# Language-model tower: the second token span's rule lookups, counts and slots moved, its groups one step later, batch 3 projected later

## The chip, the cores and the metric

The kernel runs on one core of a Trainium2 chip. The metric is the device time of one execution in microseconds, as the median of several runs. TensorE does the matrix products, VectorE (DVE) the elementwise work and reductions, ScalarE (ACT) the exponentials and most copies out of PSUM, GpSimd (POOL) the indirect DMAs and some sums, SyncE (SP) issues most of the plain DMAs.

## The reference

Tokens x [8, 512] become a hidden state h [8, 512, 64] in three layers:

```python
h = einsum('bsd,bsde->bse', emb[x], rule_transform[token_rules[x]])   # 100 rules of 64x64
xn = layernorm(h)
h = h + attention(xn)     # 8 heads, rank 32 queries and keys, values are xn, no mask, out by VO [8,64,64]
h = h + moe(layernorm(h)) # 8 experts, hidden 128, relu, the two best gates, softmax of these two
```

The layernorms have no weights. The attention is softmax(q k^T / 8) over all 512 tokens of a batch.

## The kernel before, in words

**The rules.** The token's own 64x64 matrix is the costly part of the first layer. So tokens are sorted by rule on the chip. There are NC = 32 chunks of 128 tokens (four to a batch) in NQ = 4 quarters of QC = 8 chunks. Two spans are sorted apart: span 0 is quarter 0 (batches 0 and 1), span 1 the quarters 1 to 3 (batches 2 to 7). For each quarter q:

- `fetch` (line 514, GpSimd) gathers the embedding rows with their rule number into `etok`, which lies in the tile `ctxT`; semaphore `e_got[q]`.
- `look(i, q)` (line 757, VectorE, a generator with three yields) takes the rule numbers, builds the one-hot table `oh` and each token's rank within the span.
- `count` (line 1037, TensorE) adds up `oh` over the span's chunks into two PSUM banks.
- `starts` (line 781) turns the totals into the first slot of each rule, `slots(i, q)` (line 791) gives each token its slot in `pos` (`pos_ok`), and `tile_rules` (line 814) gives the rule of each tile of 64 slots, which TensorE turns into a row (`rule_row`, line 1049) from which it reads the addresses of the matrices (`trow_ok`).
- `place` (line 520, GpSimd) scatters the rows to their slots in HBM (`emb_sorted`), waiting after every fourth for the landing.

The sorted rows come back in groups of 512 slots, 15 groups for span 0 and 19 for span 1, loaded in pairs (`load_pair`). Each group is transposed (`turn`, line 1070), copied by ScalarE to `eT`, multiplied by its rule matrices (`apply`, line 1079) and copied to `y_out`, stored, and gathered back in token order into `hbuf` (`bring`, line 532). Span 0's groups run in a loop of their own (lines 1099 to 1110 on TensorE, 843 to 848 on VectorE). Span 1's groups run inside the attention of batch 0, at the steps that `R_AT` (line 246) lists.

**The attention.** Loops over b from -2 to 8 and k from 0 to 15 make the steps (b, k), and every engine walks them in the same order. In a step TensorE computes two tiles of transposed scores (line 1193, ScalarE's exponentials behind them at line 650), two tiles of scores of a later batch for the row maxima (line 1213, VectorE's reduction at line 961), the weighted sum P.V (line 1227) and the small work that `aux_at(b, k)` lists: the transpose of the layernorm's result (`xT`), the projections (`proj`), the transposes of the maxima (`mt`), the output projection (`vo`), the experts. The maxima run LEAD = 12 steps ahead: batch nb's first two tiles stand in step (nb-1, 4). The row of negated maxima goes through SyncE's `max_row` (line 451) into row 96 of the queries, so that the transposed scores come out shifted.

**Order around the change.** Batch nb's projections are written to `qk_h` and `qk_l`, one copy for all batches; SyncE's `stack` (line 438) spreads them by DMA into `qs` and `ks`. ScalarE may overwrite `qk_h` only when all stacks of the batch before have landed (lines 711 to 714). SyncE issues in a written order (lines 463 to 487); for b = 1: the sums' row, stack(2,3), max_row(1,1), stack(3,0), stack(3,1), max_row(2,0), stack(3,2). GpSimd issues in a written order too (lines 545 to 577): fetches, scatters of span 0, fetches, `bring(0,0)`, scatters of span 1 around `values(0)`, then loads and stores of span 1's groups with `bring(0,1)` between them, and `bring(1,2)`, `bring(1,3)` behind the last store. VectorE takes the layernorm of batch 1, 2 and 3 in portions from the steps (0,0), (0,10) and (0,14) on; each begins with a wait for `hbuf` (`y_loaded`).

Of the kernel before, what the change touches and what calls it, by code (L numbers as in the profile page):

```python
# [44 lines left out]
def lm_tower_kernel(nc, ids_in, table, rules, weights, consts, out, dims):  # L45
# [33 lines left out]
    with ctx:  # L79
# [166 lines left out]
        R_AT = [(-1, 14), (-1, 15)] + [(0, g // 3) for g in range(18)]  # L246

        def x_at(nb):

            return {1: (0, 2), 2: (0, 13)}.get(nb, (nb - 2, XT))  # L250

        def proj_at(nb):

            return {1: ((0, 2), (0, 2), (0, 3), (0, 3)), 2: ((0, 14), (0, 14), (0, 15), (0, 15))}.get(
                nb, [(nb - 2, k) for k in PROJ])

        def aux_at(b, k):
# [20 lines left out]
            if k == MT[0] and 0 <= b + 1 < B:  # L278
                todo.append(("mt", b + 1, 0))
# [231 lines left out]
        def _(pool):  # L511
# [33 lines left out]
            fetch(range(FIRST + 10))  # L545
            pool.wait_ge(S["zeroed_0"], 16 * 3)
            place(0, range(FIRST))
            for c in range(FIRST + 10, NC):
                fetch((c,))
                if c % 4 == 3:  # L550
                    pool.wait_ge(e_got[c // QC], 16 * (c % QC + 1))
# [4 lines left out]
            bring(0, 0)  # L556
            pool.wait_ge(S["zeroed_1"], 16 * 4)
# [4 lines left out]
            for n in range(NP0, len(PAIRS) + AHEAD):  # L562
# [4 lines left out]
                if n == NP0 + 2:  # L567
                    bring(0, 1)
# [157 lines left out]
        def _(dve):  # L726
# [51 lines left out]
            cum, tot = bank[4][:, 0:NR], bank[5][:, 0:NR]  # L778
            more, ends, first, key = (cnt[:, i, :] for i in range(4))

            def starts(i):

                dve.wait_ge(S["ranked"], i + 1)
                link(V.tensor_scalar(cnt_i[:, 0, :], tot, 1.0, -1.0, ALU.max, ALU.add))
# [6 lines left out]
            def slots(i, q):  # L791
# [4 lines left out]
                link(V.tensor_tensor(sel[:], oh[:, c0 - lo:c1 - lo, :], key.unsqueeze(1).to_broadcast([128, QC, NR]), ALU.mult))  # L796
                link(V.tensor_reduce(slot_f[:], sel[:], AX.X, ALU.add))
                link(V.tensor_tensor(both, slot_f[:], rank[:, c0:c1], ALU.add))
                link(V.tensor_scalar(nth, both, SHIFT, (B * T >> SHIFT) - 1, ALU.logical_shift_right, ALU.bitwise_and))
                link(V.tensor_scalar(ahead, both, (B * T).bit_length() - 1, None, ALU.logical_shift_right))  # L800
                link(V.tensor_scalar(at_in, both, TS - 1, 2, ALU.bitwise_and, ALU.logical_shift_left))
                link(V.tensor_tensor(past, nth, ahead, ALU.add))
                link(V.scalar_tensor_tensor(gap, past, float(NR - 1), rule_i[:, c0:c1], ALU.add, ALU.subtract))
                link(V.scalar_tensor_tensor(past, nth, 1.0, gap, ALU.min, ALU.mult))
                link(V.tensor_tensor(tile_, past, rule_i[:, c0:c1], ALU.add))
                link(V.tensor_scalar(hi, tile_, 2, None, ALU.logical_shift_right))
# [7 lines left out]
            def tile_rules(i):  # L814
# [5 lines left out]
                V.tensor_copy(trow[:, i, :], bank[5][0:1, 0:128]).then_inc(S["trow_ok"], 1)  # L820
# [8 lines left out]
            slots(0, 0)  # L829
            tile_rules(0)  # L830
            run(look(1, 1))
# [10 lines left out]
            later = chain(look(1, 2), look(1, 3))  # L842
            for g in range(NG[0]):
# [3 lines left out]
                if 5 <= g < 9 or g >= 11:  # L847
                    next(later, None)
            run(later)
            starts(1)  # L850
            slots(1, 1)
            slots(1, 2)

# [86 lines left out]
            for b in range(-2, B + 1):  # L940
                if b == -2:
                    run(layernorm(0, "xn_ready"))
                for k in range(16):

                    if (b, k) == (-2, 9):
                        slots(1, 3)
                        tile_rules(1)
                    if k == 0 and 0 <= b - 2 < LAST - 1:
# [7 lines left out]
                    for nb, u in s_units(b, k):  # L956
# [4 lines left out]
                        V.tensor_reduce(mx[:, u // 16, u % 16:u % 16 + 1], bank[3 + n % 2][:], AX.X, ALU.max).then_inc(S["mx_done"], 1)  # L961
                    for a in aux_at(b, k):
# [70 lines left out]
        def _(pe):  # L1033
# [3 lines left out]
            def count(i, q):  # L1037
# [5 lines left out]
                for c in range(q * QC, (q + 1) * QC):  # L1043
                    M(bank[4][:, 0:NR], before[:], oh[:, c - lo, :], start=c == lo, stop=c == hi - 1)
                    last = M(bank[5][:, 0:NR], ones_bf[:], oh[:, c - lo, :], start=c == lo, stop=c == hi - 1)
# [3 lines left out]
            def rule_row(i):  # L1049

                pe.wait_ge(S["trule_ok"], i + 1)
                M(bank[5][0:1, 0:128], trule[:], ident, start=True, stop=True).then_inc(S["trowed"], 1)
# [46 lines left out]
            for g in range(NG[0] + 1):  # L1099
# [9 lines left out]
                if g in (8, 11, 13):  # L1109
                    count(1, (8, 11, 13).index(g) + 1)  # L1110
            pe.wait_ge(S["y_ok"], NG[0])

# [163 lines left out]
```

## Time and profile before

| | us |
|---|---|
| median of 3 runs | 634.21 |
| lowest, highest | 631.71, 635.44 |
| the profiled execution | 635.93 |
| its span in the trace | 633.8 |
| TensorE busy | 509.3 (80%) |
| VectorE busy | 417.5 (66%) |
| ScalarE busy | 284.7 (45%) |
| GpSimd busy | 231.3 (36%) |

The profiled execution's own time is 2.1 us more than its span. The chain that ended last goes through TensorE for 52% of the span, VectorE for 14%, GpSimd for 12% and DMAs for 7%. In the rows below the first number of a timeline row is its start and the second its length, both in us; a bracket at the end is the engine's idle time just ahead of it and what ended it.

### The profile page before, as it was taken

The page shows a single profiled execution, that of the slowest core. Times are in us where ns is not written, and L with a number is a line of the kernel's source. Part 1 is how long each engine was busy: PE and PEld are TensorE (multiplying, and loading weights), DVE is VectorE, ACT ScalarE, POOL GpSimd, SP SyncE. Part 2 cuts the span into 40 slices and gives each one's busy share as a digit, 9 for nine tenths or more (in the row PEclk, how much of TensorE's full clock was granted, in tenths as well). Part 3 has the DMA queues.
Part 4 walks back from the last instruction along what each step waited for, and adds up shares of the span by engine and source line. Part 5 has one row for each costly group of instructions (what it writes and reads, how often), then busy time and mean ns, then how long its engine had stood idle before and what let it go on. Part 6 is the DMA issues. An engine that isn't in the chain of part 4 may idle for free.

```text
span 633.8 us, 9445 instructions
## 1 busy us (share of the span) xinstructions
PE 509.3 (80%) x2732; PEld 276.6 (44%) x2732; DVE 417.5 (66%) x1026; ACT 284.7 (45%) x566; POOL 231.3 (36%) x379
## 2 busy tenths in 40 slices
PE   0178303867789897999999999999999899999684
PEld 0046301334444433445544544544554355757463
DVE  5633385734216955888778969868866876754666
ACT  0105001026555534465555565565465555386233
POOL 5764255563225200421451254133132322624512
PEclk9998655559679997999999999999999999999866
DMA  8735113733381071533320450422034000000000
GB/s 241 294 85 152 51 27 80 153 93 99 84 234 42 14 170 41 113 85 77 76 60 2 100 118 2 100 61 51 19 88 105 1 2 11 1 10 10 1 9 8
DMA packets 21935, 47.05 MB, mean 74 GB/s; under 512 B 6264, under 2 KB 11720, under 8 KB 21824
## 3 DMA queue, kind: packets, MB, share of 16 engines
q1 hardware_dynamic: 15552, 32.23, 21.0%
q0 software_dynamic: 4752, 8.20, 5.0%
q10 hardware_dynamic: 1584, 6.03, 2.9%
q8 instruction: 25, 0.41, 0.3%
q14 instruction: 22, 0.18, 0.1%
HBM read 9.97 MB, written 11.01 MB: 33 GB/s over the span
## 4 chain that ended last, share of the span: by engine, by line
PE 52%; DVE 14%; POOL 12%; issue 9%; DMA 7%; ACT 2%; SPq 2%; DVEq 0%; ACTq 0%; POOLq 0%
PE bank L1227 14%; PE bank L1213 10%; PE bank L1193 7%; POOL emb_sorted L527 5%; PE bank L1155 5%; POOL ctxT L517 4%; PE bank L1177 4%; DVE mx L961 3%; DMA ctxT<-in_table,ids 2%; PE bank L1149 2%; PE bank L1085 2%; PE bank L1150 2%; DVE r_sb L1008 2%; POOL r_sb L591 2%; DMA emb_sorted<-ctxT,pos 1%
## 5 line engine op out<-in xcount | busy, mean ns | idle before, releaser
L961 DVE TENSOR_REDUCE mx<-bank 128x1 f32<-128x512 f32 x256 | 170.5, 687 | 85.5 <-PE bank L1213 82.5
L591 POOL TENSOR_TENSOR r_sb<-r_sb 128x256 f32<-128x256 f32 x180 | 93.5, 519 | 265.5 <-DVE r_sb L1026 171.0
L650 ACT ACTIVATE prob<-bank 128x512 f32<-128x512 f32 x256 | 138.7, 597 | 58.3 <-PE bank L1193 45.7
L1213 PE MATMUL bank<-ks,qs 96*128 96x512 f32 x256 | 123.2, 489 | 10.8 <-DVE mx L961 10.5
L1227 PE MATMUL bank<-prob,xa 128*64 128x512 f32 x448 | 124.0, 633 | 0.0
L1213 PEld LDWEIGHTS bank<-ks,qs 96*128 96x128 f32 x256 | 51.1, 200 | 127.5 <-issue 107.1
L1193 PE MATMUL bank<-qs,ks 97*128 97x512 f32 x224 | 78.6, 433 | 0.0
L708 ACT ACTIVATE r_sb<-bank,stay 128x512 f32<-128x512 f32 x56 | 37.1, 686 | 44.9 <-PE bank L1150 44.7
L1193 PEld LDWEIGHTS bank<-qs,ks 97*128 97x128 f32 x224 | 38.8, 196 | 15.3 <-issue 10.5
L517 POOL DMA_INDIRECT ctxT<-in_table,ids x32 | 32.5, 1017 | 23.9 <-DMA ctxT<-in_table,ids 11.2
L527 POOL DMA_INDIRECT emb_sorted<-ctxT,pos x32 | 33.5, 1047 | 20.1 <-DMA emb_sorted<-ctxT,pos 11.7
L1227 PEld LDWEIGHTS bank<-prob,xa 128*64 128x64 f32 x448 | 22.5, 137 | 39.3 <-issue 34.9
L535 POOL DMA_INDIRECT hbuf<-y_sorted,pos x32 | 31.3, 977 | 22.4 <-DMA y_sorted<-y_out 13.7
L1085 PE MATMUL bank<-r_sb,eT 128*64 128x64 f32 (+1 forms) x544 | 28.5, 260 | 12.4 <-DVE y_out L846 11.2
L1177 PE MATMUL bank<-stay,ctxT 128*128 128x128 f32 x256 | 35.4, 285 | 0.1
L1149 PE MATMUL bank<-xs,w_h 128*128 128x512 f32 (+1 forms) x72 | 31.7, 441 | 4.6 <-DVE r_sb L1008 3.4
L1177 PEld LDWEIGHTS bank<-stay,ctxT 128*128 128x128 f32 x256 | 34.0, 200 | 2.2 <-ACT negm L719 0.4
L714 ACT CAST qk_h<-bank 128x512 fp32r<-128x512 f32 x32 | 18.4, 587 | 30.8 <-PE bank L1137 23.8
L1013 DVE TENSOR_TENSOR qk_l<-bank,qk_h 128x512 fp32r<-128x512 f32 x32 | 21.7, 687 | 15.9 <-ACT qk_h L714 15.9
L1085 PEld LDWEIGHTS bank<-r_sb,eT 128*64 128x64 f32 x544 | 23.2, 165 | 20.0 <-issue 17.8
L1132 PE MATMUL bank<-cst,xn 128*128 128x128 f32 x64 | 10.7, 289 | 24.1 <-DVE xn L892 23.9
L1076 PE MATMUL bank<-cst,e_in 128*128 128x128 f32 x68 | 16.7, 338 | 16.3 <-DMA e_in<-emb_sorted 8.0
(161 smaller groups left out, 693.4 us busy)
## 6 DMA issues: line engine op xcount, KB each, us to landing
qs<-qk_h SPq DMA_DIRECT2D x64, 128.0 KB, 2.5
ks<-qk_h SPq DMA_DIRECT2D x56, 128.0 KB, 2.4
qs<-qk_l SPq DMA_DIRECT2D x32, 128.0 KB, 2.6
ks<-qk_l SPq DMA_DIRECT2D x28, 128.0 KB, 2.5
emb_sorted<-front ACTq DMA_DIRECT2D x4, 608.0 KB, 9.7
y_sorted<-y_out POOLq DMA_DIRECT2D x19, 128.0 KB, 2.2
e_in<-emb_sorted POOLq DMA_DIRECT2D x9, 256.0 KB, 3.3
emb_sorted<-front ACTq DMA_DIRECT2D x3, 640.0 KB, 9.5
```

Source lines behind the costliest of these rows:

```text
L517: nc.gpsimd.indirect_dma_start(etok[:, c, :], None, table, bass.IndirectOffsetOnAxis(ap=ids[:, 1, c:c + 1], axis=0)).then_inc(e_got[c // Q ...
L527: nc.gpsimd.indirect_dma_start(emb_sorted[i], bass.IndirectOffsetOnAxis(ap=pos[:, c:c + 1], axis=0), etok[:, c, 0:D], None).then_inc(S[f"s ...
L591: nc.gpsimd.tensor_tensor(a[:, at:at + width], src[:, 0:width], src[:, width:2 * width], ALU.add).then_inc(S["pool_chain"], 1)
L650: nc.scalar.activation(prob[:, step % NPROB, u % 2, :], bank[u % NST][:], ACT.Exp, scale=SC).then_inc(S["exp_done"], 1)
L708: nc.scalar.activation(hid_of(ab)[:, i, :], ring(a)[:, 0:x2_of(ab).shape[1]], ACT.Relu, bias=b1_f[:, i:i + 1]).then_inc(S["relu_done"], 1)
L961: V.tensor_reduce(mx[:, u // 16, u % 16:u % 16 + 1], bank[3 + n % 2][:], AX.X, ALU.max).then_inc(S["mx_done"], 1)
L1085: last = M(out_[half * TS:(half + 1) * TS, c * D:(c + 1) * D], eT[:, g % 2, col:col + TS], r_sb[:, at_:at_ + D] if isinstance(at_, int) el ...
L1149: M(o, w1_h[:, i * HID:(i + 1) * HID], x2, start=True, stop=False)
L1177: last = M(out_[:, pair * 128:(pair + 1) * 128], ctxT[:, b % 2, pair, i * 128:(i + 1) * 128], vo_blk[:, pair, :, :].rearrange("p t e -> p ...
L1193: last = M(bank[u % NST][:], keys[:, h, :], qs[:, ub % 2, h, :], start=True, stop=True)
L1213: M(bank[3 + n % 2][:], qs[0:96, nb % 2, h, tt * 128:(tt + 1) * 128], ks[0:96, nb % 2, h, :], start=True, stop=True).then_inc(S["s_ps"], 1)
L1227: last = M(bank[5][64 * hh:64 * hh + 64, :], xa[:, b % XAR, ut, :], prob[:, step, hh, :], start=(ut == 0), stop=(ut == J - 1))
```

## The change

Fetches: eight, a wait for their landing, six more, then span 0's scatters, then the other eighteen in batches that end at chunks 17, 21, 25, 29 and 31. `bring(0,1)` directly follows `bring(0,0)`. VectorE: look 1 leaves its place ahead of the weights and looks 1 and 2 are spread over the groups 2 to 5 and 8 on; look 3 follows the last group. `slots` becomes a generator; slots 2 is split over the steps (-2,1), (-2,2), (-2,5) and (-2,9), and slots 3 over the first reductions of maxima. TensorE counts quarters 1 to 3 behind all groups of span 0, into banks 0 and 1 in place of 4 and 5. Span 1's groups stand in (0,1) to (0,7) in place of (-1,14) to (0,5). The first half of batch 0's maxima is transposed in (-1,11), behind tile 16, in place of (-1,13). Batch 3's transpose stands in (1,7) in place of (1,4), and its four projections in (1,8) to (1,11) in place of (1,5) to (1,8).

```diff
-        R_AT = [(-1, 14), (-1, 15)] + [(0, g // 3) for g in range(18)]
+        R_AT = [(0, 1 + g // 3) for g in range(20)]
...
-            return {1: (0, 2), 2: (0, 13)}.get(nb, (nb - 2, XT))
+            return {1: (0, 2), 2: (0, 13), 3: (1, 7)}.get(nb, (nb - 2, XT))
...
-            return {1: ((0, 2), (0, 2), (0, 3), (0, 3)), 2: ((0, 14), (0, 14), (0, 15), (0, 15))}.get(
+            return {1: ((0, 2), (0, 2), (0, 3), (0, 3)), 2: ((0, 14), (0, 14), (0, 15), (0, 15)), 3: ((1, 8), (1, 9), (1, 10), (1, 11))}.get(
                 nb, [(nb - 2, k) for k in PROJ])
...
                 todo.append(("gate", b - 2, 0))
-            if k == MT[0] and 0 <= b + 1 < B:
+            if (b, k) == (-1, 11) or k == MT[0] and 0 <= b < B - 1:
                 todo.append(("mt", b + 1, 0))
...
-            fetch(range(FIRST + 10))
+            fetch(range(QC))
+            pool.wait_ge(e_got[0], 16 * QC)
+            fetch(range(QC, QC + 6))
             pool.wait_ge(S["zeroed_0"], 16 * 3)
             place(0, range(FIRST))
-            for c in range(FIRST + 10, NC):
+            for c in range(QC + 6, NC):
                 fetch((c,))
-                if c % 4 == 3:
+                if c % 4 == 1 or c == NC - 1:
                     pool.wait_ge(e_got[c // QC], 16 * (c % QC + 1))
...
             bring(0, 0)
+            bring(0, 1)
             pool.wait_ge(S["zeroed_1"], 16 * 4)
...
                     load_pair(pool, n)
-                if n == NP0 + 2:
-                    bring(0, 1)
                 for g in PAIRS[n - AHEAD] if n >= NP0 + AHEAD else ():
...
-            cum, tot = bank[4][:, 0:NR], bank[5][:, 0:NR]
             more, ends, first, key = (cnt[:, i, :] for i in range(4))
...
                 dve.wait_ge(S["ranked"], i + 1)
+                cum, tot = bank[4 - 4 * i][:, 0:NR], bank[5 - 4 * i][:, 0:NR]
                 link(V.tensor_scalar(cnt_i[:, 0, :], tot, 1.0, -1.0, ALU.max, ALU.add))
...
                 link(V.tensor_tensor(sel[:], oh[:, c0 - lo:c1 - lo, :], key.unsqueeze(1).to_broadcast([128, QC, NR]), ALU.mult))
+                yield
                 link(V.tensor_reduce(slot_f[:], sel[:], AX.X, ALU.add))
+                yield
                 link(V.tensor_tensor(both, slot_f[:], rank[:, c0:c1], ALU.add))
...
                 link(V.tensor_scalar(at_in, both, TS - 1, 2, ALU.bitwise_and, ALU.logical_shift_left))
+                yield
                 link(V.tensor_tensor(past, nth, ahead, ALU.add))
...
                 link(V.tensor_tensor(tile_, past, rule_i[:, c0:c1], ALU.add))
+                yield
                 link(V.tensor_scalar(hi, tile_, 2, None, ALU.logical_shift_right))
...
                 dve.wait_ge(S["trowed"], i + 1)
-                V.tensor_copy(trow[:, i, :], bank[5][0:1, 0:128]).then_inc(S["trow_ok"], 1)
+                V.tensor_copy(trow[:, i, :], bank[5 - 4 * i][0:1, 0:128]).then_inc(S["trow_ok"], 1)
...
             starts(0)
-            slots(0, 0)
+            run(slots(0, 0))
             tile_rules(0)
-            run(look(1, 1))
             dve.wait_ge(S["w_h"], 3)
...
-            later = chain(look(1, 2), look(1, 3))
+            later = chain(look(1, 1), look(1, 2))
             for g in range(NG[0]):
...
                 V.tensor_copy(y_out[:, g % 4, :], bank[2 + g % 2][:, 0:4 * D]).then_inc(S["y_ok"], 1)
-                if 5 <= g < 9 or g >= 11:
+                if 2 <= g < 6 or g >= 8:
                     next(later, None)
             run(later)
+            run(look(1, 3))
             starts(1)
-            slots(1, 1)
-            slots(1, 2)
+            run(slots(1, 1))
...
                     run(layernorm(0, "xn_ready"))
+                    later = slots(1, 2)
                 for k in range(16):
...
                     if (b, k) == (-2, 9):
-                        slots(1, 3)
+                        run(later)
                         tile_rules(1)
+                        later = slots(1, 3)
+                    if (b, k) in ((-2, 1), (-2, 2), (-2, 5)):
+                        next(later, None)
                     if k == 0 and 0 <= b - 2 < LAST - 1:
...
                         V.tensor_reduce(mx[:, u // 16, u % 16:u % 16 + 1], bank[3 + n % 2][:], AX.X, ALU.max).then_inc(S["mx_done"], 1)
+                        next(later, None)
                     for a in aux_at(b, k):
...
                 for c in range(q * QC, (q + 1) * QC):
-                    M(bank[4][:, 0:NR], before[:], oh[:, c - lo, :], start=c == lo, stop=c == hi - 1)
-                    last = M(bank[5][:, 0:NR], ones_bf[:], oh[:, c - lo, :], start=c == lo, stop=c == hi - 1)
+                    M(bank[4 - 4 * i][:, 0:NR], before[:], oh[:, c - lo, :], start=c == lo, stop=c == hi - 1)
+                    last = M(bank[5 - 4 * i][:, 0:NR], ones_bf[:], oh[:, c - lo, :], start=c == lo, stop=c == hi - 1)
                 if c == hi - 1:
...
                 pe.wait_ge(S["trule_ok"], i + 1)
-                M(bank[5][0:1, 0:128], trule[:], ident, start=True, stop=True).then_inc(S["trowed"], 1)
+                M(bank[5 - 4 * i][0:1, 0:128], trule[:], ident, start=True, stop=True).then_inc(S["trowed"], 1)
...
                     apply(g - 1, bank[2 + (g - 1) % 2])
-                if g in (8, 11, 13):
-                    count(1, (8, 11, 13).index(g) + 1)
             pe.wait_ge(S["y_ok"], NG[0])
+            for q in range(1, NQ):
+                count(1, q)
...
                                 pe.wait_ge(S["exp_done"], u - NST + 1)
+                            else:
+                                pe.wait_ge(S["trow_ok"], 2)
                             keys = ks[:, ub % 2, :, ut * 128:(ut + 1) * 128]
...
                                 h = 2 * pair + u % 2
...
```

## Rows read from the trace of the kernel before

**Rows 1.** Busy time by stretch: PE, PEld, DVE, ACT, POOL, then the granted clock and DMA.

```profile
135.00:204.00 69.00, 58.25 (x452) 32.03 (x454) 25.14 (x51) 38.97 (x91) 25.33 (x38) 0.83 0.43 116
...
250.00:530.00 280.00, 273.43 (x1234) 136.89 (x1234) 222.75 (x499) 155.89 (x290) 87.48 (x173) 1.00 0.27 61
```

**Rows 2.** Timeline of the first span's groups: VectorE's fourth lookup, TensorE's next group.

```profile
70.11 0.72 DVE L763 CAST rule<-ctxT 128x8 f32<-128x8 int32 x1 [11.17 <-DMA ctxT<-in_table,ids]
...
72.04 1.12 PE L1085 MATMUL bank<-r_sb,eT 128*64 x16 [10.69 <-DVE y_out L846]
```

**Rows 3.** Timeline, GpSimd: the last span-0 scatter, and first issues of two batches of fetches.

```profile
39.62 0.97 POOL L527 DMA_INDIRECT emb_sorted<-ctxT,pos  x1 [0.30 <-issue]
...
54.69 0.95 POOL L517 DMA_INDIRECT ctxT<-in_table,ids  x1 [3.07 <-DMA ctxT<-in_table,ids]
...
63.79 0.95 POOL L517 DMA_INDIRECT ctxT<-in_table,ids  x1 [4.37 <-DMA ctxT<-in_table,ids]
...
70.07 0.74 POOL L552 MEMSET xa<- 128x768 f32 x1 [1.57 <-DMA ctxT<-in_table,ids]
```

**Rows 4.** Timeline, VectorE, from the totals to the first reduction of maxima.

```profile
78.95 0.25 DVE L784 TENSOR_SCALAR cnt_i<-bank 128x100 int32<-128x100 f32 x1
...
85.73 0.99 DVE L796 TENSOR_TENSOR sel<-oh,cnt 128x800 f32<-128x800 bf16 x1
...
90.95 0.42 DVE L866 TENSOR_REDUCE ln_s<-hbuf 128x4 f32<-128x256 f32 x1
...
104.05 0.69 DVE L1013 TENSOR_TENSOR qk_l<-bank,qk_h 128x512 fp32r<-128x512 f32 x1 [0.16 <-ACT qk_h L714]
...
111.70 1.29 DVE L961 TENSOR_REDUCE mx<-bank 128x1 f32<-128x512 f32 x2 [0.45 <-PE bank L1213]
```

**Rows 5.** Timeline, GpSimd: scatter of chunk 16 and the loads of span 1's first groups.

```profile
100.89 0.97 POOL L527 DMA_INDIRECT emb_sorted<-ctxT,pos  x1 [1.45 <-DMA emb_sorted<-ctxT,pos]
...
131.49 2.25 POOL L393 DMA_DIRECT2D e_in<-emb_sorted  x3 [1.46 <-DMA emb_sorted<-ctxT,pos]
```

**Rows 6.** Timeline, TensorE: first group of span 1, first transposed scores.

```profile
134.89 0.66 PE L1076 MATMUL bank<-cst,e_in 128*128 128x128 f32 x2 [6.23 <-DMA e_in<-emb_sorted]
135.21 1.20 PE L1193 MATMUL bank<-qs,ks 97*128 97x512 f32 x2
```

**Rows 7.** Timeline, TensorE: P.V of the steps (0,1), (0,2), (0,6) and (0,7).

```profile
146.49 1.08 PE L1227 MATMUL bank<-prob,xa 128*64 128x512 f32 x4
...
153.13 1.08 PE L1227 MATMUL bank<-prob,xa 128*64 128x512 f32 x4
...
192.49 1.08 PE L1227 MATMUL bank<-prob,xa 128*64 128x512 f32 x4
...
194.64 1.08 PE L1227 MATMUL bank<-prob,xa 128*64 128x512 f32 x4
```

**Rows 8.** Timeline: last store of span 1, and VectorE's start of layernorm 2.

```profile
192.37 0.54 POOL L398 DMA_DIRECT2D y_sorted<-y_out  x1 [0.40 <-ACT y_out L676]
...
201.41 0.42 DVE L866 TENSOR_REDUCE ln_s<-hbuf 128x4 f32<-128x256 f32 x1 [0.23 <-DMA hbuf<-y_sorted,pos]
```

**Rows 9.** Timeline, TensorE and ScalarE: P.V of (1,6), (1,7), (1,8) and the stall.

```profile
234.22 1.08 PE L1227 MATMUL bank<-prob,xa 128*64 128x512 f32 x4
...
240.41 0.58 ACT L714 CAST qk_h<-bank 128x512 fp32r<-128x512 f32 x1 [6.97 <-DMA ks<-qk_l]
...
241.77 0.59 PE L1172 MATMUL bank<-cst,srow 8*128 8x8 f32 x4 [5.57 <-DVE qk_l L1013]
...
243.87 1.98 PE L1227 MATMUL bank<-prob,xa 128*64 128x512 f32 x4
...
247.97 1.08 PE L1227 MATMUL bank<-prob,xa 128*64 128x512 f32 x4
```

**Rows 10.** Timeline: SyncE's max row of batch 2, and the scores that need it.

```profile
263.49 0.52 SPq L454 DMA_DIRECT2D qs<-negm  x1
...
266.84 0.71 PE L1193 MATMUL bank<-qs,ks 97*128 97x512 f32 x2
```

## The prediction

> **What bounds the kernel now.** I read the page's forty slices first, then busy time by stretch, then the chain that ended last, then the timeline engine by engine. "Step (b,k)" is one pass of the loops over b and k; the weighted sum P.V (line 1227) runs once per step, so its starts are the clock hand of everything behind 135 us. "Maxima" are the tiles of line 1213 and their reductions of line 961.
>
> From 250 us on TensorE is busy 273 of 280 us at the full 2.4 GHz; from 135 to 204 it is busy 58 of 69 us at a granted 0.83 [rows 1]. So the steady part gives nothing back: what the change can win lies ahead of 250 us, and a gain there reaches the end only if it passes every later wait. In order of time there are five such places.
>
> - The span-0 groups stop for 10.7 us, because VectorE waits 11.2 us in the fourth lookup for `e_got[3]` with a finished group's copy behind it [rows 2].
> - VectorE runs starts, two slots and the first layernorm in a row up to 96 us, then the third slots and the tile rules behind the projections; the first reduction of maxima is at 111.70 [rows 4].
> - At (-1,14) TensorE waits 6.2 us for the second span's first rows; the first transposed scores start behind it at 135.21 [rows 6].
> - The last second-span group is stored at 192.37, and VectorE starts layernorm 2 in step (0,10) at 201.41, 0.2 us after it was free: this wait is just not late now [rows 8].
> - In step (1,5) ScalarE waits 7.0 us before it may overwrite `qk_h` for batch 3, since batch 2's stacks still read it; TensorE is idle 5.6 us and its next P.V takes 1.98 instead of 1.08 us, the mark of 1.2 GHz [rows 9].
>
> **Part 1, the fetches (GpSimd queue).** Before: 18 fetches, 8 scatters, 14 fetches in batches with a wait for landing. After: 14 fetches, 8 scatters, then 18 fetches in batches of 4, 4, 4, 4, 2. GpSimd is free earlier, so the scatters begin with `pos_ok` (28.7 us) and end some 0.6 us earlier than the 40.6 us that the last one's row gives [rows 3]. A batch with its landing takes 9.1 us (54.69 to 63.79) or, with the DMA engines nearly alone, 6.3 us (63.79 to 70.07) [rows 3]. I take the mean, 7.7: 40.3 + 4 x 7.7 = 71.1, then two issues (1.3) and a landing (3.5) give `e_got[3]` at 76 instead of 70. The ends are 40.3 + 4 x 6.3 + 4.8 = 70 and 40.3 + 4 x 9.1 + 4.8 = 81.5. This is the largest unknown, -6 to +5.5 us, and most of what follows shifts with it one for one.
>
> **Part 2, the first span.** The lookup steps now follow groups 2 to 5 and 8 on. The step behind group 5 ends look 1 and runs into look 2, which waits for `e_got[2]`: chunk 23 is issued near 58 us and lands near 61. So a stall stays, from about 54.8 to 61.3, 6.5 instead of 10.7 us. Nine groups follow, some at the slow pace of 1.7 us, the last at 1.05: copied out near 72.5 instead of 79. But nothing uses that directly: look 3 now starts with `e_got[3]` at 76. From there: look 3.3 us, the last count 0.6 behind it, starts 1.8 and one slots 5.2 (85.73 to 90.95 in rows 4) give 86.9, where layernorm 0 begins, against 90.95: 4.1 us earlier. `hbuf` is there in time (store of group 14 near 76, four gathers from 77.5, landed near 84). `bring(0,1)` goes from 134 to 83 us and costs nothing, since the scatters behind it need `pos_ok` at 87 anyhow.
>
> **Part 3, up to the first scores.** The four projections follow layernorm as before, so the last `qk_l` (104.05) comes at about 100.2. Two slots steps (2.0 us) lie where VectorE waited 1.9 us for ScalarE; ends -0.2 and +0.5 us, I take +0.1. The rest of slots 2 (2.0 us) and the tile rules (1.5) still stand ahead of the rule row, and the first stack lands 5 us behind the projections, so the first reduction starts near 106.7 instead of 111.70 [rows 4]. Slots 3 (5.2 us) are now spread over the first five reductions: these take 8.2 us, the next eleven 0.82 us each as now, and tile 16 is done near 123.9. The max row leaves at once, for its transpose now stands in (-1,11); its round trip (2.0 us of DMA) ends at 127, while TensorE does six tiles more (4.9 us) and starts the transposed scores near 129.2, against 135.21: 6.0 us earlier [rows 6].
>
> **Part 4, the groups one step later.** Scatter 16 leaves at 102.9 with `pos_ok` instead of 100.89, and by the same spacing of 30.6 us [rows 5] the first loads go at 133.5 and land near 137. TensorE comes to the first group in (0,1) near 138, so the 6.2 us wait is gone, with 1 us to spare (ends: 0 and 3 us of wait). But 5 of 20 group turns that stood ahead of P.V(0,1) now stand behind it, and the last stands in (0,7) behind two more plain steps of 2.15 us [rows 7]. In numbers: P.V(0,1) near 137.0 (part of it still at the slow clock); a step with three groups is 6.6 us (146.49 to 153.13), so P.V(0,2) is at 143.6; the same four steps with the same projections cost 39.4 (153.13 to 192.49), so P.V(0,6) is at 183.0 and P.V(0,7) at 189.6; two turns more, and the last store goes near 192.8, against 192.37 [rows 8]. So the 6.0 us are spent: layernorm 2 starts at 201.8 and not 201.41, +0.4 us. What is late next is the same wait: VectorE reaches (0,10) near 198 and now waits 3 to 4 us there, with the reductions of (0,10) queued behind it and TensorE behind these.
>
> **The clock.** Behind 5.6 us of idle TensorE ran at 1.2 GHz for about one step and a half [rows 9]. Behind the new wait of 3 to 4 us I take 1.5 us of loss, with ends 0 (clock stays) and 3 (two steps at 4.3 instead of 2.7, as VectorE is the slower there). The Trainium skill, "TensorE: Matmul & The Clock Gate", section "HAM oscillation — how this bites in real kernels", speaks against this part of the change: waits for data between bursts bring the array back to half rate each time. By it the upper end would hold, and the sum would be 1.5 us less good. The trace agrees for the wait of 5.6 us; it has no wait of 3 to 4 us between dense stretches.
>
> **Part 5, batch 3 projected later.** Its transpose goes from (1,4) to (1,7), its projections from (1,5..8) to (1,8..11). P.V(1,6) to P.V(1,8) takes 13.75 us now [rows 9]; two plain steps with the rt transposes and the batch transpose are 2 x 2.15 + 0.5 + 0.35 = 5.2, and the projection work of 0.55 a step is only moved. So 8.1 us go. The stacks land at 240.3; without the stall (1,8) is reached near 240, so ends 0 and 1 us of rest. What is late next: `qk_lo` of batch 3 then comes 8.4 us ahead of (1,15), and SyncE must issue twelve stack DMAs (7.5 us) before it sends the max row, which takes 0.5 + 1.8 us. The scores of (1,15) wait for it, while today the row left at 263.49 for a start at 266.84 [rows 10]. I take 1.3 us (0 to 3). Part 5 is -6.8, between -4 and -8.
>
> **Sum.** +0.4 (layernorm 2) + 1.5 (clock) - 6.8 = -4.9 us against the profiled execution's 635.93: 631.0. That execution lies 1.7 above the median of 634.21, on which a new median will be measured, so I predict 629.4 us.
>
> **The rivals.**
> - Early fetches, 625: batches cost 6.3 us, as with quiet DMA engines, and the maxima are less DVE-bound. Layernorm 2 starts 4 to 6 us earlier. For it: the first batches run while VectorE stalls the stores; against: the one batch beside stores took 9.1. Chance 0.20.
> - Late groups, 633.5: batches cost 8.5 to 9, or the first span-1 loads are late, and layernorm 2 starts 4 us later, giving back the half of part 5. Chance 0.22.
> - The edit of part 5 doesn't clear the stall, because batch 2's stacks are later against (1,8) or ScalarE's wait only moves: half of 8.1 stays, 633.4. It is for that the stacks need SyncE's 24 issues, against it the 240.3 landing. In the 0.22 above.
> - Slower, 638: the clock in batch 0. From 135 to 204 TensorE is busy 58 us at a mean of 0.83, which is 48 us of work at 2.4 GHz [rows 1]. The turns stand in steps as dense as before, but ahead of them the steps (0,0) and (0,1) are thinner; if the clock stays down longer, at a mean of 0.73, the same 48 us take 66, 8 us more. Then layernorm 2 starts 8 us later: -4.9 + 8 = +3. It decides from 7 us on, when all of part 5 is eaten. Against it: from (0,1) on three turns a step follow each other as they do now. Chance 0.10.
> - The forecast, 627 to 632: 0.48.
>
> **How the numbers follow.** Shifting the fetches between their ends gives 629.4 - 6 = 623.4 and 629.4 + 5.5 = 634.9; with the clock's and part 5's ends added in part I say 622.5 to 635.5, leaving the slow-clock case out above. 0.5% is 3.2 us, about what a measurement can tell: below 631.0 is faster. Early fetches (0.20) and five sixths of the forecast (0.40) are there; the late groups' lower tail adds a little: 0.62 faster, 0.28 same, 0.10 slower.
>
> **What the changed profile would show.** `e_got[3]` (VectorE's fourth lookup) at 76, a VectorE stall behind group 5 near 55 to 61, layernorm 0 at 87, the first reduction near 107, the first transposed scores near 129 with no 6 us wait, the last group store near 193, a VectorE wait on `hbuf` in (0,10), no wait of ScalarE on `ks<-qk_l` behind 235, and a short wait ahead of the scores of (1,15). If `e_got[3]` is at 70 or 82, if the last store is off 192.8 by more than 3 us, or if a wait on the stacks stays, the prediction is wrong there.

## The result: slower by 0.6%, and what the profile after shows

| | before | after |
|---|---|---|
| median of 20 runs each | 635.78 | 637.57 |
| lowest, highest | 629.32, 646.58 | 634.30, 642.99 |
| ratio after / before, 95% interval | | 1.0063 (1.0040 to 1.0085) |
| profiled execution, its span | 635.93, 633.8 | 635.24, 633.4 |

The ratios here and below are taken without disturbed (slow) runs, of which before had more, while medians are of all runs: these differ by only 1.8 us, 0.3%. The forecast was 629.4, between 622.5 and 635.5. The two traces end within 0.4 us of each other, so the loss itself is not in this pair of traces; where the expected gain went can be read from it.

Busy time by stretch (as [rows 1]): from 135 to 204 TensorE is busy 5.6 us less than before, at a granted clock of 0.90 against 0.83 (part of the smaller busy time is that clock itself); from 204 to 250 the clock is 0.85 against 0.93 before.

```profile
135.00:204.00 69.00, 52.64 (x448) 28.09 (x444) 23.15 (x48) 37.43 (x89) 22.64 (x34) 0.90 0.39 109
204.00:250.00 46.00, 38.95 (x139) 17.88 (x139) 29.59 (x61) 20.23 (x39) 4.63 (x6) 0.85 0.32 73
250.00:530.00 280.00, 271.95 (x1227) 136.23 (x1225) 221.77 (x497) 155.90 (x291) 88.09 (x174) 1.00 0.27 61
```

VectorE's timeline through the span-0 groups and after them (answers [rows 2] and [rows 4]): look 2 waits only 1.0 us, the last group's copy is at 74.02 and look 3 right behind it; layernorm 0 starts at 84.59 instead of 90.95, the first reduction of maxima at 106.03 instead of 111.70.

```profile
59.49 0.17 DVE L764 CAST rule<-ctxT 128x8 f32<-128x8 int32 x1 [1.00 <-DMA ctxT<-in_table,ids]
...
74.02 0.42 DVE L850 COPY y_out<-bank 128x256 f32<-128x256 f32 x1 [0.42 <-PE bank L1094]
74.36 0.16 DVE L764 CAST rule<-ctxT 128x8 f32<-128x8 int32 x1
...
84.59 0.42 DVE L870 TENSOR_REDUCE ln_s<-hbuf 128x4 f32<-128x256 f32 x1
...
106.03 0.69 DVE L969 TENSOR_REDUCE mx<-bank 128x1 f32<-128x512 f32 x1 [3.71 <-PE bank L1224]
```

GpSimd (answers [rows 3] and [rows 5]): a fetch batch takes 6.6 us (55.63 to 62.26), not 7.7; the fetches have landed at 72.58. Scatter 16 and the first loads:

```profile
55.63 0.95 POOL L517 DMA_INDIRECT ctxT<-in_table,ids  x1 [1.73 <-DMA ctxT<-in_table,ids]
...
62.26 0.95 POOL L517 DMA_INDIRECT ctxT<-in_table,ids  x1 [1.90 <-DMA ctxT<-in_table,ids]
...
72.58 0.74 POOL L554 MEMSET xa<- 128x768 f32 x1 [1.46 <-DMA ctxT<-in_table,ids]
...
101.33 0.96 POOL L527 DMA_INDIRECT emb_sorted<-ctxT,pos  x1 [2.21 <-DVE pos L816]
...
129.98 2.94 POOL L393 DMA_DIRECT2D e_in<-emb_sorted  x4 [1.47 <-DMA emb_sorted<-ctxT,pos]
```

TensorE (answers [rows 6] and [rows 7]): the first transposed scores stand at 127.66 instead of 135.21, the first group without a wait, then P.V of (0,1), (0,2), (0,7) and (0,8).

```profile
127.66 1.05 PE L1204 MATMUL bank<-qs,ks 97*128 97x512 f32 x2
...
134.49 1.08 PE L1238 MATMUL bank<-prob,xa 128*64 128x512 f32 x4
...
135.83 0.60 PE L1085 MATMUL bank<-cst,e_in 128*128 128x128 f32 x4
...
139.81 1.08 PE L1238 MATMUL bank<-prob,xa 128*64 128x512 f32 x4
...
183.63 1.08 PE L1238 MATMUL bank<-prob,xa 128*64 128x512 f32 x4
...
187.90 1.08 PE L1238 MATMUL bank<-prob,xa 128*64 128x512 f32 x4
```

The last store and layernorm 2 (answers [rows 8]): the store is 4.6 us earlier than before. VectorE's wait ahead of layernorm 2 is 4.57 instead of 0.23 us; TensorE waits 4.64 us behind it, and its next P.V takes 1.97 instead of 1.08 us.

```profile
187.78 0.54 POOL L398 DMA_DIRECT2D y_sorted<-y_out  x1 [0.40 <-ACT y_out L677]
...
196.86 0.42 DVE L870 TENSOR_REDUCE ln_s<-hbuf 128x4 f32<-128x256 f32 x1 [4.57 <-DMA hbuf<-y_sorted,pos]
...
198.81 0.57 PE L1224 MATMUL bank<-ks,qs 96*128 96x512 f32 x1 [4.64 <-DVE mx L969]
199.31 1.97 PE L1238 MATMUL bank<-prob,xa 128*64 128x512 f32 x4
```

Batch 1 (answers [rows 9] and [rows 10]), TensorE's P.V of (1,6), the scores of (1,7), P.V of (1,7) and (1,8), the scores of (1,15); then SyncE's two max rows:

```profile
229.56 1.08 PE L1238 MATMUL bank<-prob,xa 128*64 128x512 f32 x4
...
236.74 1.22 PE L1204 MATMUL bank<-qs,ks 97*128 97x512 f32 x2 [5.29 <-DMA qs<-negm]
...
238.32 1.98 PE L1238 MATMUL bank<-prob,xa 128*64 128x512 f32 x4
...
243.08 1.98 PE L1238 MATMUL bank<-prob,xa 128*64 128x512 f32 x4
...
266.68 0.73 PE L1204 MATMUL bank<-qs,ks 97*128 97x512 f32 x2 [1.01 <-DMA qs<-negm]
...
228.33 1.35 SPq L470 DMA_DIRECT2D srow<-ctxT  x2
...
234.08 0.59 SPq L448 DMA_DIRECT2D ks<-qk_l  x1
234.72 0.59 SPq L454 DMA_DIRECT2D qs<-negm  x1
...
264.50 0.59 SPq L454 DMA_DIRECT2D qs<-negm  x1
```

Here is the answer. ScalarE's wait for the stacks is gone, as forecast, but the scores of (1,7) wait 5.29 us for `qs<-negm`: max row (1,1), which SyncE can send only behind batch 2's 24 stack DMAs and the sums' row. Before, SyncE issued the same row at 238.56:

```profile
238.56 0.59 SPq L454 DMA_DIRECT2D qs<-negm  x1
```

With the 1.98 us that such a row takes to land it stood ready at 240.5, while TensorE was held until 241.77 by `qk_h`. There were two waits of nearly one length, one behind the other's back. The changed kernel's chain that ended last says it in order of time: it runs through SyncE's issues from 221 to 234.7.

```profile
220.30 0.60 ACT prob L651
221.34 0.59 SPq L445
...
227.69 0.59 SPq L448
228.33 0.70 SPq L470
229.07 1.86 DMA srow<-ctxT
...
234.72 1.98 DMA qs<-negm
236.74 1.22 PE bank L1204 x2
```

### The profile page after: what moved, and what is told of

It reads as the page before. It is cut to its first block, busy times and chain, and to the rows that moved or that the text cites. A ratio compares the mean times of both kernels' runs of the same rounds, so it can differ in the third digit from the quotient of the medians.

```text
span 633.4 us, 9456 instructions
## 1 busy us (share of the span) xinstructions
PE 509.5 (80%) x2732; PEld 275.7 (44%) x2732; DVE 416.8 (66%) x1026; ACT 285.0 (45%) x566; POOL 231.7 (37%) x379
## 4 chain that ended last, share of the span: by engine, by line
PE 56%; DVE 18%; issue 9%; DMA 5%; POOL 5%; SPq 3%; ACT 3%; another core or an unknown queue 1%; ACTq 0%; DVEq 0%; POOLq 0%
PE bank L1238 14%; PE bank L1224 11%; PE bank L1204 7%; PE bank L1164 5%; DVE mx L969 4%; PE bank L1186 4%; PE bank L1094 3%; PE bank L1158 2%; PE bank L1159 2%; DVE r_sb L1017 2%; PE bank L1085 2%; SPq L445 2%; SPq L448 2%; POOL r_sb L592 2%; DMA ks<-qk_l 2%
## 5 line engine op out<-in xcount | busy, mean ns | idle before, releaser
L1238 PE MATMUL bank<-prob,xa 128*64 128x512 f32 x448 | 125.3, 639 | 0.0
L517 POOL DMA_INDIRECT ctxT<-in_table,ids x32 | 32.8, 1024 | 23.5 <-DMA ctxT<-in_table,ids 11.1
L1094 PE MATMUL bank<-r_sb,eT 128*64 128x64 f32 (+1 forms) x544 | 27.1, 251 | 10.7 <-ACT eT L634 6.2
L1094 PEld LDWEIGHTS bank<-r_sb,eT 128*64 128x64 f32 x544 | 22.1, 158 | 18.3 <-issue 9.5
L1164 PE MATMUL bank<-r_sb,stay 128*64 128x512 f32 x112 | 27.8, 606 | 1.6 <-ACT r_sb L709 1.0
L1159 PE MATMUL bank<-xs,w_l 128*128 128x512 f32 (+1 forms) x72 | 28.2, 393 | 0.0
```

The source lines that it names most:

```text
L1094: last = M(out_[half * TS:(half + 1) * TS, c * D:(c + 1) * D], eT[:, g % 2, col:col + TS], r_sb[:, at_:at_ + D] if isinstance(at_, int) el ...
L1159: M(o, w1_l[:, i * HID:(i + 1) * HID], x2, start=False, stop=True).then_inc(S["up_ps"], 1)
L1164: last = M(out_[64 * t:64 * t + 64, 0:x2_of(b).shape[1]], w2_f[:, 2 * i + t, :], hid_of(b)[:, 2 * i + t, :], start=True, stop=True)
L1238: last = M(bank[5][64 * hh:64 * hh + 64, :], xa[:, b % XAR, ut, :], prob[:, step, hh, :], start=(ut == 0), stop=(ut == J - 1))
```

## The experiments

Times are against the kernel before in the same comparison, as medians, with the ratio and its interval. Two kernels of different comparisons are set against each other only by way of their own "before beside it".

| kernel | median | before beside it | ratio (95%) |
|---|---|---|---|
| batch 3's move alone | 634.05 | 634.74 | 0.990 (0.980 to 0.999), from 3 of its 6 runs |
| the same again | 634.81 | 632.71 | 1.003 (1.000 to 1.007) |
| changed, without batch 3's move | 634.94 | 634.74 | 1.002 (0.998 to 1.006) |
| changed, again | 637.44 | 634.74 | 1.004 (1.000 to 1.007) |
| before, again | 633.50 | 632.62 | 1.002 (0.999 to 1.005) |
| changed, row (1,1) first | 630.89 | 634.74 | 0.994 (0.991 to 0.997) |
| before, batch 3's move and row first | 627.32 | 632.71 | 0.991 (0.989 to 0.994) |
| changed, row first, groups one step earlier | 623.06 | 632.71 | 0.985 (0.982 to 0.989) |
| the same, row (2,0) early too | 623.10 | 632.71 | 0.986 (0.983 to 0.989) |
| changed, row first, key stacks by GpSimd | 632.69 | 632.62 | 0.999 (0.995 to 1.003) |
| changed without batch 3's move, key stacks by GpSimd | 633.95 | 632.62 | 1.004 (1.001 to 1.007) |
| before, key stacks by GpSimd | 633.17 | 632.62 | 0.997 (0.993 to 1.001) |

From the traces, three marks: P.V of (0,0), the start of layernorm 2, and the stretch from there to P.V of (2,4), all in us.

| trace | P.V (0,0) | layernorm 2 | from there to P.V (2,4) |
|---|---|---|---|
| before | 140.2 | 201.4 | 77.1 |
| before, again | 137.9 | 200.8 | 76.8 |
| batch 3's move alone | 135.1 | 193.4 | 79.0 |
| the same again | 137.7 | 203.6 | 78.6 |
| before, batch 3's move and row first | 136.9 | 197.5 | 73.8 |
| changed | 130.8 | 196.9 | 81.4 |
| changed, again | 131.9 | 198.1 | 82.3 |
| changed, without batch 3's move | 130.4 | 199.9 | 78.1 |
| changed, row first | 131.7 | 200.2 | 74.7 |
| changed, row first, groups one step earlier | 130.8 | 198.4 | 72.1 |
| the same, row (2,0) early too | 132.0 | 194.6 | 72.5 |
| changed, row first, key stacks by GpSimd | 132.5 | 201.0 | 74.5 |
| changed without batch 3's move, key stacks by GpSimd | 131.5 | 200.7 | 78.7 |

From P.V (2,4) to the end all of them take 353.5 to 356.8 us, so what is won or lost up to there reaches the end.

**Batch 3's move alone**, twice.

```diff
-            return {1: (0, 2), 2: (0, 13)}.get(nb, (nb - 2, XT))
+            return {1: (0, 2), 2: (0, 13), 3: (1, 7)}.get(nb, (nb - 2, XT))
...
+            ... 3: ((1, 8), (1, 9), (1, 10), (1, 11))}.get(
```

> The kernel before with the move of batch 3 alone (its transpose in (1,7), its projections in (1,8) to (1,11)). Theory A, the prediction's part 5: ScalarE's wait for the stacks in (1,5) was the stall, so it goes and the time falls by 4 to 8 us. Theory B, from the changed kernel's trace: behind it stands a second wait of nearly the same length, the scores of (1,7) for the max row (1,1), which SyncE sends behind batch 2's 24 stack DMAs; the old stall only covered it and gave cover to the projections beside it. Then TensorE waits 4 to 5.5 us in (1,7) for the row, three projections and a max-row wait of about 1 us come on top in (1,8) to (1,15), and the time is 0 to 3 us above the kernel before.

> The kernel before with batch 3's move alone, once more, since its first time was uncertain (interval 0.980 to 0.999) and its trace had started layernorm 2 at 193.4 us on code that is that of the kernel before. By the traces the stretch from layernorm 2 to P.V of (2,4) is 79.0 against 77.0 us, so 1 to 3 us above the kernel before. If it is 3 us or more below, batch 3's move does win something that the traces' stretches don't show.

TensorE of the first of the two:

```profile
226.04 1.08 PE L1227 MATMUL bank<-prob,xa 128*64 128x512 f32 x4
...
233.27 1.22 PE L1193 MATMUL bank<-qs,ks 97*128 97x512 f32 x2 [5.25 <-DMA qs<-negm]
...
234.85 1.98 PE L1227 MATMUL bank<-prob,xa 128*64 128x512 f32 x4
...
238.84 1.08 PE L1227 MATMUL bank<-prob,xa 128*64 128x512 f32 x4
...
253.82 0.47 PE L1213 MATMUL bank<-ks,qs 96*128 96x512 f32 x1 [0.73 <-DVE mx L961]
...
260.80 0.72 PE L1193 MATMUL bank<-qs,ks 97*128 97x512 f32 x2 [1.06 <-DMA qs<-negm]
```

On the code of before, the move alone makes the 5.25 us wait for the max row in (1,7), the 0.73 us wait for VectorE and the 1.06 us wait in (1,15). The stretch is 79.0 and 78.6 against 77.1 and 76.8: the move costs 1.9 us in the mean. The first time, by its ratio some 6 us below before, would even fit theory A, but it rests on three runs; the second gives a loss of 0.3%, with an interval (0.9998 to 1.0065) that just includes none. The first trace started layernorm 2 at 193.4, on code that is that of before up to there. So the times of this kernel decide little. Theory A falls by the traces, in which the scores of (1,7) wait 5.25 and 5.31 us, and by the next experiment.

**The changed kernel without batch 3's move** (the same lines the other way).

> The changed kernel with batch 3's transpose and projections back where they were. Theory A: the stall of (1,5) comes back and the time rises by 4 to 8 us over the changed kernel. Theory B: SyncE's issues set the end of that stretch either way, so the upstream lead of 3.7 us at P.V of (1,0) is now kept to the end: 1 to 4 us below the changed kernel and 0 to 3 us below the kernel before. P.V of (1,6) to (1,7) takes near 9.7 us, and no wait for the max row stands ahead of the scores of (1,15).

ScalarE's timeline of this kernel, then TensorE's, in batch 1:

```profile
240.16 0.58 ACT L715 CAST qk_h<-bank 128x512 fp32r<-128x512 f32 x1 [7.43 <-DMA ks<-qk_l]
...
241.52 0.59 PE L1181 MATMUL bank<-cst,srow 8*128 8x8 f32 x4 [6.03 <-DVE qk_l L1022]
```

The old stall is back, and the time falls by 2.5 us against the changed kernel beside it (634.94 against 637.44), where theory A wanted it 4 to 8 us higher. So the move costs some 2 to 2.5 us, and all the other changes together come out at the level of before: 1.002. It isn't 0 to 3 us below before, as I expected; the lead of 3.7 us in the first trace was not typical.

**The row ahead of stack(2,3).**

```diff
+                if b == 1:
+                    max_row(b, 1)
                 if 0 <= b + 1 < B:
                     stack(b + 1, 3)
-                if 0 <= b < B:
+                if 0 <= b < B and b != 1:
                     max_row(b, 1)
```

> The changed kernel, with SyncE sending max row (1,1) ahead of stack(2,3) instead of behind it. Theory B: the row leaves near 231 instead of 234.7, so the scores of (1,7) wait 1 to 2 us instead of 5.3; stack(2,3) lands 2 to 3 us later, near 239, which ScalarE may feel for up to 2 us in (1,8). 1 to 3 us below the changed kernel. Rival: the wait is not the row but the stacks' landing, then nothing changes or it gets slower by the 2 us.

SyncE's timeline of this kernel (the sums' row, then max row (1,1)), then TensorE's:

```profile
231.84 1.35 SPq L470 DMA_DIRECT2D srow<-ctxT  x2
234.46 0.56 SPq L454 DMA_DIRECT2D qs<-negm  x1
...
236.33 0.88 PE L1206 MATMUL bank<-qs,ks 97*128 97x512 f32 x2 [1.37 <-DMA qs<-negm]
```

One small DMA moved ahead of six others on one queue: the wait is 1.37 us instead of 5.29, no wait on the stacks shows, and the kernel is 6.5 us below the changed one beside it. That is more than twice the 3 us that I expected at most, and it matches the stretch (74.7 against 81.4 and 82.3): the wait is 3.9 us shorter, and the granted clock is 0.50 from some 237 to 240 only, against 233 to 247 in the changed kernel's first trace. The order on SyncE's queue is shown to be the cause. What is left of the wait comes from the sums' row: SyncE sends the max row only when that row, issued at 231.84, has landed.

**The same on the kernel before**, with batch 3's move (both edits above).

> The kernel before with batch 3's move and with max row (1,1) ahead of stack(2,3), but with nothing of the other changes. If the upstream changes win nothing at the end (theory C), this equals the changed kernel with the row sent first, that is 3 to 5 us below the kernel before, or is up to 1.5 us better. If the upstream lead is real and kept, it is 3 to 4 us above that kernel.

5.4 us below before, and 1.5 us better against its own neighbour than the row with all the upstream changes (3.9): the upper end of what theory C gave. So the upstream changes, as they stand, win nothing.

**Both kernels again**, unchanged, for a second trace.

> The changed kernel once more, for a second trace and for its time beside the others of this comparison: 0 to 4 us above the kernel before. Open is where the time differs from one execution to the next, since the two first traces have spans within 0.4 us of each other. If the lead at layernorm 2 (196.9 against 201.4 us) is typical, it is there again within 1 us; the rival is that the first trace was a lucky one and layernorm 2 starts at 199 or later.

> The kernel before once more, for a second trace. The lead of the changed kernel at layernorm 2 (its two traces: 196.9 and 198.1 us) was taken against one trace of before, 201.4. The kernel with batch 3's move alone has the same code up to there and started layernorm 2 at 193.4. So I expect 193 to 202 here: near 193 to 198 says that the changed kernel has no lead there as a rule, near 201 that it has one of about 3 us.

The changed kernel's second trace starts layernorm 2 at 198.1, between the two cases that I had set (within 1 us of 196.9, or 199 and later). Before's second trace starts it at 200.8, which by my own expectation spoke for a lead of 3 us; with all traces taken together there is none. The mark of layernorm 2 on code with the upstream part of before: 201.4, 200.8, 193.4, 203.6, 197.5, mean 199.3. With the changed upstream part: 196.9, 198.1, 199.9, 200.2 and, in two further traces, 201.0 and 200.7, mean 199.5. At the first P.V the lead is there in every trace (137.6 against 131.5 in the mean, 6 us), at layernorm 2 the means are equal. The single traces lie between 193.4 and 203.6 and between 196.9 and 201.0, so five and six of them can't exclude a difference of 2 or 3 us; the times of the kernel without batch 3's move (1.002) and of the one above speak against a lead.

**Groups one step earlier.**

```diff
-        R_AT = [(0, 1 + g // 3) for g in range(20)]
+        R_AT = [(0, g // 3) for g in range(20)]
```

> The changed kernel with max row (1,1) sent first, and span 1's groups in (0,0) to (0,6) instead of (0,1) to (0,7). Theory C: in every trace of the changed upstream part VectorE waits 4.4 to 4.6 us in (0,10) for hbuf, because the last group stands two plain steps later; the lead of 6 us at the first P.V is spent there, and TensorE comes out of it at the slow clock. One step earlier the last store comes about 2 us earlier, the wait falls to 0.5 to 2.5 us, and the time is 1 to 3 us below the kernel with the row sent first alone. Rival: the loads land too late for (0,0) (133.3 us against 132), so that step takes the wait, the clock falls there, and nothing is won.

VectorE's and TensorE's timeline of this kernel at layernorm 2:

```profile
198.35 0.42 DVE L872 TENSOR_REDUCE ln_s<-hbuf 128x4 f32<-128x256 f32 x1 [2.42 <-DMA hbuf<-y_sorted,pos]
...
200.31 0.47 PE L1226 MATMUL bank<-ks,qs 96*128 96x512 f32 x1 [2.49 <-DVE mx L971]
```

The wait at (0,10) is 2.4 instead of 4.6 us, and the time is 9.7 us below before (623.06, ratio 0.985): better than both kernels. Against the row first alone, each by its own before, it is 5.8 us better, where I expected 1 to 3. In this trace and that of the next experiment layernorm 2 starts at 198.4 and 194.6 (mean 196.5, against 199.5), and from there to P.V (1,0) it takes 17.7 us in both, against 18.3 to 21.5 with the later groups. That is some 4 of the 5.8 us, from two traces and across two comparisons; the rest I can't place. P.V (1,6) to (1,8) took 6.7 us here, as the clock stayed at 1.00 behind the wait for the row, but 8.3 in the next experiment's trace and 8.2 with the later groups: this is no gain of the edit. The loads don't hold the first group at (0,0): it starts at 133.6 with no wait of note. ScalarE waits 1.88 us for a stack in (1,8), which holds up nothing that shows.

**Row (2,0) early too.** `max_row(2, 0)` is moved ahead of `stack(3, 1)`.

> As the groups one step earlier with row (1,1) first, and in addition SyncE sends max row (2,0) ahead of stack(3,1). The wait of 1.0 us ahead of the scores of (1,15) goes: 1 us below that kernel, 4 to 7 us below the kernel before. If stack(3,1) is now late for anything, it shows as a wait on ks in (2,12) and the gain is gone.

The wait at (1,15) is gone from the trace and the step is 1.2 us shorter, P.V (1,14) to (1,15) being 3.0 instead of 4.2. The median is the same, 623.10, and so is the stretch, 72.5 against 72.1, since this trace has the slow clock behind the wait in (1,7) and the other hasn't. 1 us is below what six runs can tell, so the edit is unproven.

**Key stacks by GpSimd**, in three kernels.

```diff
-                for s, src in enumerate((qk_h, qk_h, qk_l) if b else ()):
+                for s, src in enumerate((qk_h, qk_h, qk_l) if b and b != 2 else ()):
...
+                if b == 0:
+                    pool.wait_ge(S["qk_lo"], 12)
+                    for g in range(4):
+                        pool.wait_ge(S["exp_done"], 8 * (g + 1))
+                        for s, src in enumerate((qk_h, qk_h, qk_l)):
+                            pool.dma_start(ks[32 * s:32 * s + 32, 0, 2 * g:2 * g + 2, :].bitcast(F32),
+                                           src[32 * g:32 * g + 32, 2:4, :].bitcast(F32)).then_inc(key_in[g], 16)
...
```

> The changed kernel with max row (1,1) ahead of stack(2,3), and batch 2's twelve key stacks issued by GpSimd, which has nothing to do there, instead of by SyncE. If SyncE's issues are what sets the stretch from P.V (1,6) to (1,8), the scores of (1,7) wait under 1 us (5.3 in the changed kernel, 1.4 with the row first alone) and ScalarE waits for no stack in (1,8): 5 to 9 us below the changed kernel. Rival: the 128 KB stacks are limited by their transfer and not by who issues them; then it is level with the row sent first alone, 6 to 7 us below the changed kernel, or GpSimd's own order delays it to a loss.

> The changed kernel without batch 3's move, and with batch 2's key stacks issued by GpSimd. Batch 2's stacks have landed near 236 instead of 240, so ScalarE's wait in (1,5) falls from 7 to 2 or 3 us: 4 to 6 us below the same kernel with SyncE issuing all. Rival as before: nothing changes if the transfer and not the issue is the limit.

> The kernel before with nothing changed but batch 2's key stacks issued by GpSimd. The double stall of (1,5) and (1,7) had one cause, 24 issues on one queue, so half of the issues taken away shortens both: 4 to 6 us below the kernel before. If it is level with the kernel before, the two waits aren't set by SyncE's issues.

All three missed: the times are within 0.4% of before, and the kernel with the row first isn't better for it (0.999, against 0.994 without). SyncE's timeline of that kernel while batch 2's stacks are sent, and GpSimd's line behind its twelve stacks:

```profile
224.32 1.90 SPq L446 DMA_DIRECT2D qs<-qk_l  x1
226.27 4.21 SPq L446 DMA_DIRECT2D qs<-qk_h  x2
230.53 2.02 SPq L446 DMA_DIRECT2D qs<-qk_l  x1
...
227.76 1.03 POOL L538 DMA_INDIRECT hbuf<-y_sorted,pos  x1 [0.30 <-issue]
```

Busy time of both kernels from 224 to 228 (columns as in [rows 1]; first with GpSimd, then with the row first alone):

```profile
224.00:228.00 4.00, 4.00 (x16) 1.75 (x16) 3.62 (x8) 1.72 (x4) 3.70 (x9) 1.00 0.95 197
```

```profile
224.00:228.00 4.00, 4.00 (x16) 1.62 (x16) 3.04 (x5) 2.31 (x5) 0.39 (x1) 1.00 0.85 197
```

GpSimd sends its twelve in 5.9 us, but SyncE's own issues stretch meanwhile: two of them take 4.21 us where they take 1.2 otherwise. In the stretch in which both queues send nothing but stacks, the DMA engines move 197 GB/s with one queue and with two; they are busy 0.85 of the time with SyncE alone, and 0.95 with both. That speaks for the rival of the first expectation, that the transfer and not the issue is the limit. The wait for the row is 1.36 us with GpSimd (and 0.77 for the sums' row just ahead of it) and 1.37 without, and the stretches to P.V (2,4) are level (74.5 and 74.7). Without batch 3's move, ScalarE's wait for the stacks is 5.68 instead of 7.43 us, so there they did land earlier, but two P.V behind it take 1.98 us instead of one, and the stretch is 78.7 against 78.1.

The test isn't clean. GpSimd works in a written order, so the edit also holds back the four gathers of `hbuf` that stand behind the stacks: they are issued at 227.8 to 232.6, beside the stacks, instead of 210.7 to 215.4. From 228 to 232 the engines move 262 GB/s with them against 210 without. What twelve issues on a second queue would bring without the gathers was not tried.

## Why the prediction was wrong, step by step

- **Part 1, fetches.** `e_got[3]` forecast at 76, landed at 72.5 (72.4 to 75.3 in the other traces of this code). The batch read above cost 6.6 us, near the lower end of 6.3. VectorE reached look 3 only at 74.36, behind the last group, which had been forecast at 72.5: two waits changed places, and layernorm 0 came at 84.6 to 86.6 in six traces against 86.9. Right in size.
- **Parts 2 and 3.** First reduction 106.0 (forecast 106.7), first transposed scores 127.7 (129.2), the 6 us wait at (-1,14) gone. Right; the lead at the first P.V is real in every trace.
- **Part 4.** "The 6.0 us are spent": layernorm 2 forecast 0.4 us later than before, found 0.2 us later in the mean of the traces. The first trace alone, 4.6 us earlier and with its last store at 187.8 instead of 192.8, would have called this wrong by the prediction's own sign. The new wait was forecast at 3 to 4 us and is 4.4 to 4.6. Not forecast was a wait of TensorE for a stack ahead of the maxima between P.V (0,3) and (0,4): 1.5 to 3.1 us in all six traces with the groups one step later, none in the two with the groups one step earlier. Three of the five traces with the upstream code of before have such a wait too (1.6 to 2.4 us), but not the one on which the prediction was built.
- **The clock.** Forecast 1.5 us. From layernorm 2 to P.V (1,0) the two traces of before take 17.65 us each, five of the six with the later groups 18.3 to 19.1 and the sixth 21.5: 1.4 us more in the mean. Right in size. The upper end of 3 us, which the forecast had tied to a rule of the Trainium skill ("TensorE: Matmul & The Clock Gate", section "HAM oscillation — how this bites in real kernels"), that waits for data between bursts bring the array back to its slow rate, was reached once in six. What the rule says of the single wait holds here: 1.97 instead of 1.08 us for the P.V behind the 4.64 us wait.
- **Part 5 is the step that failed.** The forecast took 8.1 us off and put back 1.3 for the max row of (1,15). That row's wait was right (1.01 us). (8.1 is not quite its own difference: 13.75 less 5.2 is 8.55.) But the stretch P.V (1,6) to (1,8) was priced as 5.2 us of plain steps, as if nothing else were late there. The text asked what is late next for (1,15) and not for (1,7), where the same queue holds max row (1,1) behind the same stacks. Measured with the move alone, in two traces against two of before: the stretch is 12.8 and 13.1 instead of 13.75 and 13.5 us, steps (1,4) to (1,6) are 0.9 us shorter, and (1,8) to (1,15) take 22.9 and 22.8 instead of 19.75. There three more projections stand (1.4 us), VectorE is late once (0.4) and the row once (1.3). Only one of the three had cost nothing before, in the stall's shadow; the others are what (1,4) to (1,6) and the stretch behind the stall are rid of. The sum of these parts is near +1.5, that of the whole stretch from layernorm 2 +1.9, instead of -6.8: over 8 us of error in one term.
- **The sum with the measured terms**: +0.2, +1.4 and +1.5 to +1.9 give +3.1 to +3.5, against +1.8 and +2.7 us of the two median pairs and 4.0 us by the ratio of 1.0063.
- **The rivals.** Both early and late groups missed; "the edit of part 5 doesn't clear the stall" was nearest, but it named the stacks, priced half of the 8.1 and got no chance of its own. The rival for slower, at 638, had nearly the number that was measured (637.57), by luck: its mechanism, a slower clock in batch 0, didn't show. The granted clock from 170 to 200 us is 0.90 to 0.98 in the six traces with the later groups, and 0.72 to 0.95 in the five with the upstream code of before.

## What to carry to other kernels

When a wait is to be removed, list for every engine what each of its next waits would need and when that is ready, and not only at the next landmark: a second wait of nearly the same length may stand behind the first, and work that lay in its shadow becomes path. In a hand-ordered DMA queue a small late transfer (here 8 KB that TensorE's next scores wait for) goes ahead of bulk that isn't due yet. And one trace is one draw: the same code began layernorm 2 anywhere between 193 and 204 us, so a lead of a few us needs several traces.

## What the runs showed of the hardware

A second issuing queue gave no more DMA throughput while both sent stacks: 197 GB/s from 224 to 228 us either way. The engines' busy share rose from 0.85 to 0.95, and the first queue's issues slowed from 0.6 to 2.1 us each.

The granted clock between 170 and 200 us was 0.89, 0.94, 0.95, 0.86 and 0.72 in five traces of one upstream code (before, before again, batch 3's move alone, with the row first, alone again), and the stretch from P.V (0,3) to (0,10) took 34.9, 36.1, 32.8, 35.0 and 39.6 us: the slowest clock goes with the longest stretch. It isn't the clock alone, for the second, fourth and fifth also have a wait of 2.4, 1.6 and 2.3 us for a stack in it. Why the same instructions are granted a different clock from one execution to the next stays open.
